# The order of TensorE's four tasks within a step of the attention loop: transposes, scores, projection products, weighing in place of scores, transposes, weighing, projection products

## The reference

```python
x = x + layernorm(attention(layernorm(x)))        # 32 heads of 64, 8 groups of keys and values, window of 256, ALiBi
x = x + layernorm(feed_forward(layernorm(x)))     # gate and up 512 -> 1408, silu, down 1408 -> 512
# attention, for each head h and token t:
scores = xq @ xk.T / 8 + bias                     # xq, xk RMS-normed; bias = slope * distance, -inf outside the window
attn   = softmax(scores)
out    = (attn @ xv) ...; return out @ wo.T
```

## Time and profile before

| | |
|---|---|
| three runs | 1304.18, 1305.19, 1307.57 us |
| the profiled execution, its own time | 1309.66 us |
| its span, first to last instruction | 1307.9 us |
| mean granted TensorE clock | 0.973 of full speed |
| first stage | to about 318 us |
| attention, pass 0 | 318.04 to 373.35 us |
| attention, passes 1 to 4 (no projection) | 373.35 to 503.98 us |
| attention, passes 5 to 15 (projection at steps 8 to 31) | 503.98 to about 960 us |
| TensorE, VectorE, ScalarE busy in the span | 93%, 73%, 58% |

### The profile page before, as it was taken

The page is one execution under the profiler, slowest core; times in us unless marked ns, Lnnn a source line. Parts: engine busy times, 40 slices in busy tenths (PEclk is TensorE's granted clock), DMA queues, the critical chain, the costliest instruction groups (busy, mean ns, idle before and its releaser), DMA issues.

```text
span 1307.9 us, 30500 instructions
## 1 busy us (share of the span) xinstructions
PE 1214.9 (93%) x9016; PEld 1019.5 (78%) x9016; DVE 954.1 (73%) x2528; ACT 761.1 (58%) x2013; POOL 369.1 (28%) x445
## 2 busy tenths in 40 slices
PE   5999999996699998999999999999989979999998
PEld 4868777784577777898888888888877768888876
DVE  4597776858889987888888888888864346546464
ACT  3545455554589887777877777777732234232330
POOL 1000000001147766445354444434421100202021
PEclk9999999997599998999999999999989989999999
DMA  4216262455555556455454554545352252101010
GB/s 155 103 73 242 114 240 113 193 213 186 232 178 170 168 168 197 130 187 166 155 181 148 187 163 154 174 152 186 126 183 97 88 185 81 65 33 65 33 65 34
DMA packets 99245, 189.03 MB, mean 145 GB/s; under 512 B 8032, under 2 KB 36832, under 8 KB 99168
## 3 DMA queue, kind: packets, MB, share of 16 engines
q1 hardware_dynamic: 99168, 188.07, 42.2%
HBM read 116.48 MB, written 71.57 MB: 144 GB/s over the span
## 4 chain that ended last, share of the span: by engine, by line
PE 63%; DVE 12%; issue 10%; DMA 6%; ACT 4%; POOL 3%; SPq 1%; DVEq 1%; POOLq 0%; ACTq 0%
PE bank L1209 17%; PE bank L1340 15%; PE bank L1277 12%; PE bank L1240 6%; PE bank L1231 6%; DVE u_sb L990 3%; DMA wo_stage<-woT 2%; PE bank L1266 2%; DVE pT_lo L997 2%; DVE inv_rms L944 2%; ACT p_sb L794 1%; PE bank L1256 1%; PE bank L1258 1%; PE bank L1257 1%; DMA o_in<-o_scr 1%
## 5 line engine op out<-in xcount | busy, mean ns | idle before, releaser
L794 ACT ACTIVATE p_sb<-u_sb,low 128x384 f32<-128x384 f32 (+2 forms) x512 | 273.8, 535 | 84.6 <-DVE low L990 57.3
L990 DVE CUSTOM_DVE_ANT_0 u_sb<-bank,bias 128x384 f32<-128x384 f32 (+2 forms) x512 | 231.5, 452 | 40.5 <-PE bank L1231 21.0
L1231 PE MATMUL bank<-k_st,q_st 128*128 128x384 f32 (+2 forms) x1024 | 252.9, 329 | 6.5 <-DVE v_out L964 2.9
L1240 PE MATMUL bank<-ident,p_sb 128*128 128x128 f32 x1152 | 225.6, 287 | 31.4 <-DVE pT_lo L997 23.1
L997 DVE TENSOR_TENSOR pT_lo<-bank,pT_hi 128x384 f16<-128x384 f32 (+2 forms) x512 | 232.0, 453 | 28.9 <-ACT pT_hi L802 18.0
L802 ACT ACTIVATE pT_hi<-bank 128x384 f16<-128x384 f32 (+2 forms) x512 | 204.2, 399 | 49.5 <-PE bank L1240 47.7
L1231 PEld LDWEIGHTS bank<-k_st,q_st 128*128 128x128 f32 x1024 | 178.7, 195 | 30.3 <-DVE low L990 4.3
L1240 PEld LDWEIGHTS bank<-ident,p_sb 128*128 128x128 f32 x1152 | 139.8, 143 | 78.0 <-ACT p_sb L794 40.1
L598 POOL TENSOR_TENSOR o_mid<-o_raw,inv_sum 128x256 f32<-128x256 f32 x128 | 82.9, 648 | 285.1 <-DVE o_raw L1011 283.8
L561 POOL TENSOR_TENSOR rstd<-var_eps,minus_half 128x1 f32<-128x1 f32 (+1 forms) x31 | 23.4, 754 | 492.1 <-DVE var_eps L888 492.1
L1256 PE MATMUL bank<-v_st,pT_hi 128*128 128x64 f16 x1152 | 156.9, 195 | 0.5 <-DVE pT_lo L997 0.5
(11 more groups left out here) (114 smaller groups left out, 2416.5 us busy)
## 6 DMA issues: line engine op xcount, KB each, us to landing
q_scr<-qk SPq DMA_DIRECT2D x64, 512.0 KB, 2.7
q_st<-q_scr SPq DMA_DIRECT2D x32, 1024.0 KB, 7.7
k_st<-k_scr SPq DMA_DIRECT2D x64, 256.0 KB, 3.0
o_scr<-o_out SPq DMA_DIRECT2D x128, 128.0 KB, 2.7
o_in<-o_scr SPq DMA_DIRECT2D x16, 1024.0 KB, 5.3
k_scr<-qk SPq DMA_DIRECT2D x16, 512.0 KB, 2.6
z_in<-z_scr SPq DMA_DIRECT2D x8, 1024.0 KB, 6.2
x_in<-x SPq DMA_DIRECT2D x4, 1024.0 KB, 8.3
```

The costliest lines, as they stand in the source:

```text
L794: nc.scalar.activation(p_sb[:, u % RING, 0:w], u_sb[:, u % RING, 0:w], ACT.Exp, scale=-1.0, bias=low[:, u % RING:u % RING + 1], accum_out= ...
L990: nc.vector.tensor_tensor_reduce(out=u_sb[:, u % RING, 0:w], in0=bank[u % 2][:, 0:w], in1=bias[:, 2 * u // UNITS, u % REP, at:at + w], sca ...
L1231: mm = nc.tensor.matmul(bank[u % 2][:, 0:w], q_st[:, s, r, P * i:P * i + P], k_st[:, s, part, P * key:P * key + w], start=(part == 0), sto ...
L1240: mm = nc.tensor.transpose(bank[2 + u % 2][:, P * j:P * j + P], p_sb[:, u % RING, P * j:P * j + P], ident[:])
```

## The change

TensorE's step is put into another order. In the table, "transpose" moves ahead of "scores"; the other engines' stages keep their order among themselves. `unit_work` of TensorE takes the kinds that it is to issue, and `attend` calls it three times, with the projection's two parts in between. A step is now: transposes of unit u-2, `transpose_o`, scores of unit u, `project_o`, weighing of unit u-4. The lags, the buffers, the semaphores and the other engines' programs stay as they are, and no instruction is added or removed.

```diff
-LAGS = {"split": 3, "scores": 0, "transpose": 2, "exps": 0, "invert_sums": 1, "weigh": 4, "take": 5}
+LAGS = {"split": 3, "transpose": 2, "scores": 0, "exps": 0, "invert_sums": 1, "weigh": 4, "take": 5}
...
-            def unit_work(n, u):
+            def unit_work(n, u, kinds=("transpose", "scores", "weigh")):
                 for stage, nn, uu in due(n, u):
                     work = {"scores": scores, "transpose": transpose_p, "weigh": weigh_values}.get(stage)
-                    if work:
+                    if stage in kinds:
                         work(nn, uu)
 
             def attend(n, tile=None):
                 for u in range(UNITS):
-                    unit_work(n, u)
+                    unit_work(n, u, ("transpose",))
                     if tile is not None:
                         m, at = divmod(u - START, STEP)
                         if m in range(4) and at == 0:
                             transpose_o(tile, m)
+                    unit_work(n, u, ("scores",))
+                    if tile is not None:
                         m, at = divmod(u - START - 4, STEP)
                         if m in range(4):
                             if m == 0 and at == 0:
...
                             project_o(tile, m, (2 * at, 2 * at + 1), bank[7])
+                    unit_work(n, u, ("weigh",))
```

## The result

The changed kernel takes 1347.51 us, the median of four runs (1344.47 to 1348.53), against 1306.38 us of the kernel before in the same set (four runs, 1304.18 to 1309.21): 1.0304 times as long, with a 95% interval of 1.0286 to 1.0322 (the interval behind every ratio below is of this kind). The profiled execution took 1346.6 us with a span of 1344.8. The forecast of 1327 us had the direction. Of the 41 us it had 22, and its range ended at 1338.

A forecast was written before the change was run, and what follows sets the result against it. It took passes 1 to 4 as bound by the latency of the units' chain over the engines, most of passes 5 to 15 by TensorE's work; 11.4 + 2.5 + 8 = 22 us gave 1327 us, range 1307 to 1338.

The forecast's parts named there:

- The loop: Transposes of u-2, scores, `add_bias`, `exps`, transposes of u: 2.43 us per two three-tile steps, 2.66 at multiples of four.
- Faster: Rival: fewer bare weight loads in projection passes, later scores covered in passes 0 to 4; -8 us, 1297; chance 0.08.
- no difference: Rival: loop and saving cancel or vanish in slack, or TensorE issues scores while waiting; 1305 us; chance 0.09.
- the clock: Rival: longer waits in passes 1 to 4 bring the clock to 1.2 GHz; 44 us more, 1370; chance 0.04.
- Passes 1 to 4: Passes without projection: 1.8 us more per half pass, 14.4 in all, less 1.5 each for passes 3 and 4: 11.4.
- The other part: Passes 3 and 4: a slower pass hides the output weights' load that `finish_o` stands behind; 1.5 us off each.
- Passes 5 to 15: Projection passes: 0.8 - 0.65 + 0.55 = 0.7 us each, eleven cost 8 (bounds -8 and 12).
- steps 0 to 10: Start of a projection pass: `add_bias` comes later behind the scores, 1.1 us, of which 0.8 reaches step 11.
- saving: Three-tile projection steps on TensorE: 1.44 us for 1.48, about 0.05 less; 0.65 us a pass from step 11 on.
- waits: Projection passes, transposes of units 12, 20, 24 behind `split_pT`: 0.2 to 0.35 us each, 0.9 without overlap, 0.55 taken.
- pass 10 over 42.5: Sign that the forecast is wrong: pass 10 over 42.5 us (or under 40.5), where about 41.8 was expected.
- The rule on weight loads: Next weights load while a matmul runs, so saving 0; the prediction instead followed the row's 0.08 us behind short products.

The follow-up runs named there:

- e1: Kernel before with the transposes moved ahead of the scores, the weighing still ahead of the products: 1351.09 us, ratio 1.034.
- e8: Kernel after with the weighing put between the transposes and the scores: 1402.59 us, ratio 1.0724.
- e6: Kernel after reordered to scores, products, weighing, transposes, `transpose_o`, with the lags of before: 1305.02 us, ratio 0.9986.
- e9: Kernel after with VectorE's `split_oT` moved to steps 6, 13, 18, 25 and its bit operations to 22, 23, 26: 1369.84 us, ratio 1.0479.
- e12: Kernel after with `split_oT` alone moved, from steps 12 and 24 to 13 and 25: 1344.31 us, ratio 1.0282.
- e2: Kernel after reordered to scores, transposes, `transpose_o`, products, weighing, so only the weighing moves against the kernel before: 1317.53 us, ratio 1.0072.
- e11: Kernel after with the new order kept in passes 0 to 4 alone, the old one in passes 5 to 15: 1323.31 us, ratio 1.0129.
- e3: Kernel after with the new order kept only in the passes with projection, the old one elsewhere: 1332.69 us, ratio 1.0187.
- e4: Kernel after with the transposes at lag 3, and split, weighing and take one step later each: 1336.34 us, ratio 1.0225.
- e7: Kernel after with the transposes at lag 3 and `split_pT` kept at lag 3: 1659.41 us, ratio 1.2696.
- e10: e6's order with e5's lags: 1304.87 us, ratio 0.9981.
- e5: Kernel before with the transposes at lag 3, and split, weighing and take one step later each: 1305.82 us, ratio 0.9984.

## Why the prediction was wrong, by its own steps

**Right: the mechanism and the direction.** The loop was named ahead of time and it is there: 2.46 and 2.70 us a turn against 2.43 and 2.66. Steps 12 to 15 of pass 2 take 5.16 us (5.09 forecast, 4.60 before), steps 0 to 3 3.97, as priced. e1 puts the whole loss on the swap of transposes and scores, e8 shows that what stands between the two is paid in full, e6 that the loss goes when the transposes are a step older. "Faster", "no difference" and "the clock" fall: the granted clock is 1.00 in each of passes 1 to 4, where before it was 0.95 in pass 4.

**Passes 1 to 4, forecast 11.4, measured 15.1: mis-sized a little.** Steps 4 to 7 take 4.13 us against 3.9 forecast, and steps 8 to 11 5.04 against 4.8. The shorter turns of two-tile units had been put together from means, without the crossing to three tiles. Steps 8 to 11 had been given two turns of 2.4, though unit 8 is a multiple of four too, and by the prediction's own rule its turn is the longer one. There is a slip in the sum as well: 3.98 + 8.7 + 5.09 is 17.8, not 17.6, so its own terms give 2.0 for a half pass. Measured, a half pass costs 2.2 to 2.4 us, not 1.8. The other part held: passes 3 and 4 took 1.5 us more than pass 2 before, and take no more than it now. Pass 0 cost 3.1 for 2.5; its mean granted clock was low in both kernels, 0.63 before and 0.65 after.

**Passes 5 to 15, forecast 8, measured 21: the step that failed.** Per pass, the prediction had 0.8 for steps 0 to 10, a saving of 0.65 and waits of 0.55 in steps 11 to 31. Pass 10 shows +1.0 and, for steps 11 to 31, +0.94 in place of -0.1. Three terms make this up.

The *saving*. TensorE in one three-tile step of the kernel after, and the next transposes:

```profile
751.75 0.53 PE L1240 MATMUL bank<-ident,p_sb 128*128 128x128 f32 x3
752.03 0.60 PE L1231 MATMUL bank<-k_st,q_st 128*128 128x384 f32 x2
752.46 0.39 PE L1277 MATMUL bank<-wo_lo,oT_hi 128*128 128x512 f32 x1
752.69 0.40 PE L1277 MATMUL bank<-wo_hi,oT_hi 128*128 128x512 f32 x1
752.93 0.20 PE L1256 MATMUL bank<-v_st,pT_hi 128*128 128x64 f16 x1
753.20 0.53 PE L1240 MATMUL bank<-ident,p_sb 128*128 128x128 f32 x3
...
755.02 0.52 PE L1240 MATMUL bank<-ident,p_sb 128*128 128x128 f32 x3 [0.19 <-DVE pT_lo L997]
```

751.75 to 753.20 is 1.45 us. Medians over such steps, start to start, from the two traces, by task:

| task | before | after | forecast |
|---|---|---|---|
| transposes | 0.327 | 0.280 | 0.28 |
| scores | 0.349 | 0.433 | 0.44 |
| products | 0.543 | 0.471 | 0.46 |
| weighing | 0.260 | 0.271 | 0.26 |
| sum | 1.479 | 1.455 | 1.44 |

Each task was right within 0.011 us, yet the saving is 0.024 for 0.05. It is a small difference of large terms. I had rounded them to hundredths, carried 1.48 less 1.44 as 0.05, and set the two unseen crossings at nothing; the first weighing product behind the long ones does take 0.01 more. About 0.3 us a pass.

The *waits* at the transposes of units 12, 20 and 24 are the main term. Taken with the neighbours that share a `transpose_o`, steps 12 to 14 grew by 0.30, steps 21 and 22 by 0.45, steps 24 to 27 by 0.51 us. Together that is 1.26 us, and a little more with the saving inside them added back; the forecast was 0.55, with 0.9 as the bound. Of the pricing two things were missing. The scores behind the transposes take 0.08 more, which I had charged to TensorE's step and to the loop, and not to these waits. And I had cut the sum from 0.9 to 0.55 for overlap, which isn't there: the wait at 755.02 above comes after a step in which TensorE had work without a gap, and no later step gives it back. "TensorE is the bound there" held for most steps; e9 and e12 show that at three units it is VectorE's work that TensorE waits for.

*Steps 0 to 10* cost 1.0 for 0.8.

The 0.2 of steps 0 to 10, the 0.3 of the saving and 0.75 for the waits are 1.25 us a pass; over the eleven passes, pass 5 with less, 13 us were missed. With 3.7 in passes 1 to 4 and 0.6 in pass 0 these are 17 of the 19 us by which the measured difference of the medians (41) exceeds the forecast one (22). The range failed at the same place: its upper bound for the projection passes was 12 us, and they cost 21. The text's own sign, "pass 10 over 42.5", came true with 43.07.

**The rule on weight loads.** By the rule of the Trainium skill that the prediction cites ("TensorE: Matmul & The Clock Gate", Part 2, the step on LDWEIGHTS) the order would have changed nothing on TensorE. The rows show that it does, in both directions: 0.024 us a step saved by the change, 0.026 lost in e2 (1.505 for 1.479), with the same instructions and no wait. The first product behind the weighing takes 0.31 where the second takes 0.23, and its weight load starts only 0.03 us ahead of it, that of the second 0.23 ahead. It looks as if the load can't be hidden behind short matmuls, but no run tried that by itself. On the size, the measurement decides.

**Pass 5** costs only 1.3 us more where passes 6 to 14 cost 1.95. The prediction said that the DMAs' cover grows, but had no term for a wait that goes by it: in the kernel before, the first `transpose_o` of all, at step 4, waits 1.38 us for the DMA that loads `o_in`. In the kernel after, in e1 and in e11, with slower passes ahead, it doesn't wait; in e3 and e2, whose passes ahead are as before, it waits 1.62 and 2.11 us, and pass 5 takes 46.5 and 45.2 us. The granted clock differs as well (0.96 before and after, 0.93 in e3, 0.92 in e2, 1.00 in e1 and e11), and no run takes the two apart.

What stays open: how the 0.4 us a pass between e1 and the kernel after divides into crossings and waits was not taken apart, and neither was the +1.0 of steps 0 to 10, for which no run was made.

## What to carry to other kernels

Before moving an instruction that waits ahead of one that doesn't, write down each ring that this closes: every chain over the engines that comes back to the waiting instruction, its length divided by the steps it spans. There is one through the data (here transposes, scores, `add_bias`, `exps`), one through each reused buffer (e4), and one through the order of two other engines (e7); a lag that opens the first may leave or make another. The way out here was to put the waiting instruction last in its step (e6), which has the same cycle on TensorE and works on older data; it is level with the kernel before, not a gain over it that these runs can tell. And where a step's saving is a few hundredths, price the places where a single step's spare time runs out, one by one and in full, before taking any of it as gain.

## What the runs showed of the hardware that was not expected

- Short and long matmuls in turn cost at the crossing, start to start at a granted clock of 1.00: a 384-column product behind 64-column f16 products takes 0.08 us more than behind 512-column ones (0.258 in e2, 0.175 in the kernel before), and the first 512-column product behind the 64-column ones 0.08 more than the second (0.314 against 0.229 in the kernel before). Behind 512-column products the first weighing product takes only 0.01 more (0.039 in the kernel after, against 0.028 behind 128-column transposes in the kernel before).
- An integer operation of VectorE with two operands in SBUF took 2.88 us instead of 0.68 beside a 2.75-us GpSimd product (e9). In the kernel before, these operations stand at steps 19 to 21; whether they were put there for this is not known, but moving them to 22, 23 and 26 cost more than it saved.
- e6, e10 and e5 are 0.14 to 0.19% faster than the kernel before, with intervals that end at 0.9997, 0.9993 and 0.9995: about 2 us, below the 0.3% that this kernel's runs were taken to tell. It isn't shown to be a gain.
